# Two reader-less products out, reciprocals of exponential sums in batches of four tiles, and the last tile finished and stored in halves

## What is computed

```python
x = x + layernorm(attn_block(layernorm(x)))          # 4 layers of convolution and feed-forward
x = x + layernorm(ffn_block(layernorm(x)))

def ffn_block(h):
    query  = h @ Wq.T
    scores = (query @ Wr.T) @ (aux_keys @ Wr.T).T / sqrt(48) + log_rel     # 128 slots
    top    = top_k(scores, 8)
    w      = softmax(query @ aux_keys[top].T / 8 + log_rel[top])
    aux    = (w @ aux_values[top]) @ Wvd.T @ Wvu.T
    gate   = ...                       # from the variance of h and a small learned net
    return h + gate * aux
```

## Time and profile before

| what | value |
|---|---|
| median of 3 runs | 204.06 us (203.06, 204.06, 204.06) |
| the profiled execution's own time | 203.3 us |
| its span, first to last instruction | 201.5 us |
| PE busy | 184.3 us (91%) |
| DVE busy | 157.3 us (78%) |
| ACT, POOL busy | 109.8 us (54%), 81.9 us (41%) |
| granted TensorE clock, mean | 0.992 |

### The profile page before, as it was taken

How to read it: one execution, slowest core, us unless ns; L and a number is a source line. 1 busy time by engine, 2 the same in 40 slices (tenths; PEclk the granted TensorE clock), 3 DMA queues, 4 the chain that set the end, 5 groups by cost and what they waited for, 6 DMA issues and landing times.

```text
span 201.5 us, 3811 instructions
## 1 busy us (share of the span) xinstructions
PE 184.3 (91%) x1235; PEld 150.2 (75%) x1235; DVE 157.3 (78%) x547; ACT 109.8 (54%) x281; POOL 81.9 (41%) x142
## 2 busy tenths in 40 slices
PE   7875898979999998999999999999999898988992
PEld 7875888848988787788998889988988444555430
DVE  6798846969887778884888786555899997998872
ACT  5287276664457458646556555453835585862210
POOL 4222417652244422442244432367462635555400
PEclk9999699999999999999999999999999999999999
DMA  4999990000000000000000000000000000002675
GB/s 112 421 405 395 415 391 26 0 5 0 0 5 0 0 3 0 0 3 0 0 0 5 0 3 0 0 3 0 2 0 2 0 3 0 2 0 109 236 280 213
DMA packets 5505, 15.31 MB, mean 76 GB/s; under 512 B 925, under 2 KB 1965, under 8 KB 4462
## 3 DMA queue, kind: packets, MB, share of 16 engines
q1 hardware_dynamic: 5486, 15.07, 19.6%
HBM read 10.87 MB, written 4.19 MB: 75 GB/s over the span
## 4 chain that ended last, share of the span: by engine, by line
PE 70%; DVE 9%; DMA 7%; ACT 4%; issue 3%; POOL 2%; SPq 2%; DVEq 0%; ACTq 0%
PE bank L1561 14%; PE bank L1449 12%; DMA XT<-in_xT 7%; PE bank L1684 7%; PE bank L1540 7%; PE bank L1513 4%; PE bank L1619 3%; PE bank L1501 3%; PE bank L1690 3%; PE bank L1489 3%; POOL RS L362 2%; PE bank L1608 2%; DVE Z L1038 1%; PE bank L1641 1%; PE bank L1526 1%
## 5 line engine op out<-in xcount | busy, mean ns | idle before, releaser
L362 POOL TENSOR_TENSOR RS<-SS,nhalf 128x4 f32<-128x4 f32 x36 | 41.5, 1163 | 63.6 <-DVE SS L1032 63.3
L1561 PE MATMUL bank<-ffst,HD 128*128 128x128 f32 x256 | 31.3, 275 | 0.0
L1561 PEld LDWEIGHTS bank<-ffst,HD 128*128 128x128 f32 x256 | 29.9, 192 | 0.5 <-issue 0.3
L1449 PE MATMUL bank<-M,XT 128*128 128x226 f32 x128 | 27.7, 362 | 0.1
L1032 DVE TENSOR_REDUCE SS<-SQ 128x4 f32<-128x260 f32 x36 | 15.2, 422 | 15.9 <-ACT SQ L646 15.3
L670 ACT ACTIVATE HD<-bank,b1r 128x512 f32<-128x512 f32 x32 | 20.2, 683 | 11.8 <-PE bank L1540 11.8
L1449 PEld LDWEIGHTS bank<-M,XT 128*128 128x128 f32 x128 | 23.2, 189 | 3.4 <-issue 3.1
L646 ACT ACTIVATE SQ<-bank 128x256 f32<-128x256 f32 x36 | 13.8, 382 | 20.1 <-PE bank L1561 11.4
L1072 DVE TENSOR_TENSOR_SCAN V<-cvst,U 128x514 f32<-128x514 f32 x16 | 20.0, 1248 | 0.0
L1489 PE MATMUL bank<-wcc,XT 128*128 128x128 f32 x128 | 16.9, 296 | 2.8 <-DMA XT<-in_xT 2.8
L1540 PE MATMUL bank<-Z,w1r 64*128 64x256 f32 x128 | 18.1, 402 | 1.0 <-ACT Z L664 0.7
(11 more groups left out here) (269 smaller groups left out, 352.3 us busy)
## 6 DMA issues: line engine op xcount, KB each, us to landing
XT<-in_xT SPq DMA_DIRECT2D x4, 1024.0 KB, 11.9
X<-in_x SPq DMA_DIRECT2D x4, 1024.0 KB, 14.4
out<-X SPq DMA_DIRECT2D x8, 512.0 KB, 2.8
w1r<-in_w1d SPq DMA_DIRECT2D x1, 516.0 KB, 16.4
lt<-in_late SPq DMA_DIRECT2D x1, 449.5 KB, 16.5
M<-in_mraw SPq DMA_DIRECT2D x1, 448.0 KB
w2r<-in_w2n SPq DMA_DIRECT2D x1, 256.0 KB, 16.8
winr<-in_win SPq DMA_DIRECT2D x1, 254.0 KB, 2.6
```

Of the source, the lines that this page charges most:

```text
L362: pool.tensor_tensor(RS[:, g, :], SS[:, g, :], nhalf[:, :], ALU.pow).then_inc(done, 1)
L1449: last = pe.matmul(x_bank(t), XT[:, g, c, j * P:(j + 1) * P], M[:, c, PADS:MW], start=(c == 0), stop=(c == VC - 1))
L1561: last = pe.matmul(HK[g][:, j * P:(j + 1) * P], HD[:, u % 2, a, at:at + P], ffst[:, L, a * P:(a + 1) * P], start=False, stop=True, skip_gr ...
```

## The change

PE drops one product of the third `keep_busy` and the whole fourth one. DVE takes the reciprocals only in the odd calls of `dots`, for four tiles at once, and `mix` counts them accordingly. The last tile (15) is multiplied in two halves of 256 columns into two banks (OB[1] and the free SB[0]), finished by DVE in two halves, and stored in two halves of 128 KB; tile 14 gets a store of 256 KB of its own.

```diff
--- before.py
+++ after.py
@@ -312,10 +312,16 @@
                     sp.dma_start(wr_s[:, :], wr).then_inc(s_late, 16)
                     sp.dma_start(kds[:, :], kd).then_inc(s_late, 16)
                     sp.dma_start(SWR[:, :], srow).then_inc(s_rel, 16)
-            for k in range(PAIRS):
+            for k in range(PAIRS - 1):
                 sp.wait_ge(out_ready, 2 * k + 2)
                 sp.dma_start(out_v[k], X[:, 2 * k:2 * k + 2, :]).then_inc(s_out, 16)
-            sp.wait_ge(s_out, 16 * PAIRS)
+            sp.wait_ge(out_ready, TILES - 1)
+            sp.dma_start(out_v[PAIRS - 1][:, 0:1, :], X[:, TILES - 2:TILES - 1, :]).then_inc(s_out, 16)
+            for h in range(2):
+                sp.wait_ge(out_ready, TILES + h)
+                sp.dma_start(out_v[PAIRS - 1][:, 1:2, h * HC:(h + 1) * HC],
+                             X[:, TILES - 1:TILES, h * HC:(h + 1) * HC]).then_inc(s_out, 16)
+            sp.wait_ge(s_out, 16 * (PAIRS + 2))
 
         @block.gpsimd
         def _(pool):
@@ -498,7 +504,7 @@
                 if i == 0:
                     pool.wait_ge(k2_done, 4)
                 pool.wait_ge(dots_done, b // 2)
-                pool.wait_ge(es_inv, b // 2)
+                pool.wait_ge(es_inv, i + 1)
                 link(pool.tensor_tensor(gs, RES[:, a:b], GA[:, 4, a:b], ALU.mult))
                 link(pool.tensor_tensor(w, gs, XQ[:, a:b, 1], ALU.mult))
                 link(pool.tensor_tensor(w, w, XQ[:, a:b, 0], ALU.add))
@@ -1289,7 +1295,8 @@
                     dve.wait_ge(dots_done, k - 1)
                 dve.tensor_tensor(DQ[:, k % 2], AY[:, a:b, :], YB.rearrange("p (t n) -> p t n", t=2),
                                   ALU.mult).then_inc(dots_in, 1)
-                dve.reciprocal(RES[:, a:b], ES[:, a:b]).then_inc(es_inv, 1)
+                if k % 2:
+                    dve.reciprocal(RES[:, a - 2:b], ES[:, a - 2:b]).then_inc(es_inv, 1)
                 dve.wait_ge(dots_in, k + 1)
                 dve.tensor_reduce(XQ[:, a:b, :], DQ[:, k % 2].rearrange("p t (i d) -> p t i d", i=2), AX.X,
                                   ALU.add).then_inc(dots_done, 1)
@@ -1301,6 +1308,15 @@
                 dve.tensor_tensor(F[:, a:b, 0:ZD + 1], F[:, a:b, 0:ZD + 1], rows(GX[:, 6, a:b], b - a, ZD + 1), ALU.mult)
                 dve.tensor_tensor(F[:, a:b, 96:P], AY[:, a:b, VB:2 * VB], rows(GX[:, 7, a:b], b - a, VB),
                                   ALU.mult).then_inc(f_done, 1)
+
+            def finish_last():
+
+                t = TILES - 1
+                for h, bank in enumerate((OB[1], SB[0])):
+                    a, b = h * HC, (h + 1) * HC
+                    dve.wait_ge(o_mm, t + h + 1)
+                    dve.scalar_tensor_tensor(out=X[:, t, a:b], in0=X[:, t, a:b], scalar=GX[:, 5, t:t + 1],
+                                             in1=bank[:, a:b], op0=ALU.mult, op1=ALU.add).then_inc(out_ready, 1)
 
             def finish(t):
 
@@ -1390,7 +1406,7 @@
             finish(12)
             finish(13)
             finish(14)
-            finish(15)
+            finish_last()
 
         @block.tensor
         def _(pe):
@@ -1682,6 +1698,15 @@
                 else:
                     pe.wait_ge(qt_done, PAIRS)
                 pe.matmul(OB[t % 2][:, :], FT[:, t // 2 % 2, (t % 2) * P:(t % 2 + 1) * P], FM[:, :], start=True,
+                          stop=True).then_inc(o_mm, 1)
+
+            def output_last():
+
+                pe.wait_ge(ft_ready, PAIRS)
+                pe.wait_ge(out_ready, TILES - 2)
+                pe.matmul(OB[1][:, 0:HC], FT[:, 1, P:2 * P], FM[:, 0:HC], start=True, stop=True).then_inc(o_mm, 1)
+                pe.wait_ge(sc_read, TILES)
+                pe.matmul(SB[0][:, HC:2 * HC], FT[:, 1, P:2 * P], FM[:, HC:2 * HC], start=True,
                           stop=True).then_inc(o_mm, 1)
 
             def keep_busy(n):
@@ -1734,11 +1759,10 @@
             turn_q(4)
             scores(1)
             scores(2)
-            keep_busy(3)
+            keep_busy(2)
             mean_sum()
             turn_q(5)
             scores(3)
-            keep_busy(1)
             turn_e(0, 0)
             turn_q(6)
             memory(0)
@@ -1784,7 +1808,7 @@
             output(12)
             output(13)
             output(14)
-            output(15)
+            output_last()
 
 
 def kernel(**inputs):
```

## The result

The changed kernel takes 201.21 us (median of 20 runs, 200.61 to 203.49) against 203.81 for the kernel before (20 runs, 201.37 to 208.04). The forecast was 202.2. The ratio is 0.9907, with an interval of 0.9884 to 0.9929, or about 1.9 us less; it leaves out two slow executions of the kernel before (208.02 and 208.04 us). The medians are 2.6 us apart, and the profiled executions have spans of 201.5 and 199.4 us, 2.1 apart. The sum in the prediction was 1.8.

A forecast was written before the change was run, and what follows sets the result against it. DVE was taken as the bound, its only hole a 1.2 us wait ahead of dots(0). Terms of 1.25 + 0 + 0.55 = 1.8 us off the median of 204.06 gave 202.26, forecast as 202.2 us, range 201.0 to 203.5.

The forecast's parts named there:

- The sum: Whole kernel: 1.25 us from products, 0 from reciprocals and 0.55 from the last tile make 1.8 us less.
- The number: Whole kernel: forecast time of 202.2 us, from a median of 204.06 for the kernel before; chance 0.60.
- Dropped products: PE ahead of turn_e(0): reached 1.8 us earlier, so dots(0) on DVE starts 1.25 us earlier.
- `mean_sum` earlier: DVE's reader of mean_sum: one product less ahead of it gains nothing, at most some hundredths of a us.
- Reciprocals: DVE in dots: four of eight go, but they lie in the product's shadow, so 0 us.
- The rival of 0.48 us: DVE in dots: reciprocals were on the path, four at 0.12 us give another 0.48 us, 201.7 us; chance 0.08.
- Lasting to the tail: From dots(0) to the tail: the 1.25 us gain lasts, with turn_f(0) at 176.35 us in place of 177.60.
- Last tile: End of kernel: DVE ends 0.1 us earlier and stores start earlier, 0.55 us in all, ends 0 and 0.7.
- the rate of 1 KB rows: Last stores: may be slower than 2 KB rows at 387 GB/s; taken nearer the full rate.
- The clock: PE tail after 176 us: TensorE's clock falls without the products, one spell costing 1.7 us; chance 0.08.

The follow-up runs named there:

- e2: Kernel before with only the product between scores(3) and turn_e(0) dropped; ratio 0.9965 (0.9935 to 0.9994).
- e3: Kernel before with only the third of the three products ahead of mean_sum dropped; ratio 0.9974 (0.9944 to 1.0005).
- e8: Kernel before with two products in place of one between scores(3) and turn_e(0); ratio 1.0082 (1.0051 to 1.0112).
- e5: Kernel before with only the reciprocals changed, in batches of four tiles; ratio 0.9999 (0.9965 to 1.0034).
- e9: Kernel before with two more, unread reciprocals in each of the eight calls of dots, three in all; ratio 1.003 (0.9983 to 1.0076).
- e6: Kernel before with tiles 14 and 15 stored apart, each whole; ratio 0.9977 (0.9942 to 1.0012).
- e1: Kernel before with only the two products dropped, reciprocals and tail unchanged; median of six runs 202.85 us, against 203.22 for the kernel before.
- e12: Kernel before with only the two products dropped, run a second time; median of twelve runs 201.80 us, ratio 0.9921 (0.9879 to 0.9964).
- e11: The changed kernel itself, run once more for more executions and another trace; 201.44 us, ratio 0.9913 (0.9870 to 0.9955).
- e7: Changed kernel without its other five reader-less products; median of six runs 210.10 us, against 203.37 for the kernel before.

## Why the prediction was right, point by point

**The number.** The forecast of 202.2 started from a median of three runs, 204.06; that of twenty is 203.81. The measured 201.21 lies 1.0 us below the forecast, and most of this is not the change. The change took 2.1 us in the profiled executions (201.23 against the 201.5 forecast for one), and about as much group by group (203.2 at a clock of 0.992 against 201.1 at 0.988 to 0.991; 204.0 against 202.0 at 0.983). The medians differ by 2.6 because that of before, 203.81, has a time like those of its slower group (0.983) beside the experiments, and the changed kernel's comes from the faster of its two. What the prediction missed in mechanism is 0.3 us, the difference between 2.1 and 1.8.

**Dropped products, 1.25 us: right, mechanism and size.** 1.59 - 0.34 = 1.25 on the row, and e2, e3 and e8 show the slope of 0.8 to 0.9 us per product and the point where DVE's own list takes over.

**`mean_sum` earlier, nothing: slightly mis-sized.** Counted as some hundredths at most; counted from select(0) it is 0.07 or 0.18 us, 0.07 in the changed kernel's first trace. It does not come from `mean_sum` itself: its reader starts 0.34 us behind the reduction before (165.25, 165.59) and after (165.35, 165.69). It comes behind the reader, and looks like a hold of select(3) by PE. In all seven traces with three products the first maximum of select(3) starts 0.03 or 0.04 us behind the end of scores(3) (166.57 and 166.60 before), in the changed kernel 0.88 behind it (165.70 and 166.58), and from that maximum to the reduction it is 1.44 or 1.45 us with three products and 1.37 or 1.38 with two. But no row names a wait for scores(3), so this cause is not shown.

**Reciprocals, 0 us: right.** The reduction starts 0.03 us behind the product with or without one, in the changed kernel and in e5. The rival of 0.48 us is refuted, and e9 shows that its unit price was double the real one. The Trainium skill (VectorE: DVE Perf Modes, "The DRAIN you can't avoid") says that the next operation does not start until the pipeline has emptied, and excepts one that is not held. In e9 the three reciprocals start within 0.13 us though one takes 0.15, so here the exception describes them and not the rule.

**Lasting to the tail: right.** The chain reaches the tail at 176.15 (176.35 forecast), with the tail's own duration the same.

**Last tile, 0.55 us: right in sum.** 0.65 by the table (20.64 + 2.61 against 20.71 + 3.19). DVE is done 0.07 us earlier behind turn_f(0) (0.1 forecast), but with the data flowing without a hole this does not count. The reason given, the early start of tile 14's data, is what e6 shows by itself. The unknown, the rate of 1 KB rows, was 340 GB/s against 387, near the end that I took.

**The sum.** 0.19 + 1.25 + 0.11 + 0.65 make up the 2.20 us of the table (36.25 - 34.05), 0.08 of the 0.11 being the MATCH_REPLACE8 of select(5). 0.12 of the 0.19 belongs ahead of select(2), where the changed kernel's trace is behind by 0.10 us. So the change itself took 0.07 + 1.25 + 0.11 + 0.65, about 2.1 us, as the spans say.

**The clock, 0.08: the rival I underrated.** It did not decide the changed kernel's median, but the mechanism is real and near. Two traces of the two products alone have it, at 1.55 and 1.57 us; I had priced one spell at 1.7 and said that no idle gap went beyond half a microsecond; the one ahead of turn_f(0) was 0.57 us in the kernel before and is 0.84 in e1. Why both profiled executions of e1 and e12 have the fall and those of the changed kernel and e11 have not is not settled: their gap is 0.83 and 0.81, and PE is as busy around it. The Trainium skill (TensorE: Matmul & The Clock Gate, "HAM oscillation") describes PE re-throttling after idle gaps; the falls here came after gaps of 0.17 and 0.84 us, and stayed away after gaps of 0.17 and 0.83.

## What to carry to other kernels

When a product without a reader is taken out, find first who waits for the engine behind it: here it was worth its length until the list of DVE became the limit, and no more. Such products can also hold the clock up: without the other five it fell for thirty microseconds. Where PE waits anyway a product costs nothing; that one there prevents a fall is not shown. At the end of a kernel, storing the last finished tile at once gained as much as cutting the last tile in two as well; and operations that wait for the one ahead leave a shadow in which small ones cost nothing.

## What was not expected of the hardware

The clock can stay at 1.2 GHz for thirty microseconds with PE busy 27.47 of 30 us (e7), once it has fallen after a stretch at 0.57 of 2; in e1 and e12 it was back at 1.00 after some three. And a store of one tile in two halves needed 0.45 us per issue on the queue of SP, where a whole tile or pair needed 0.34 to 0.37.
